# Background ticks of the top-k attention: none in the first maxima pass of the plain attention, more in the wide attention

## The chip, the cores and the metric

One core of a Trainium2 chip runs the whole program. The metric is the device time of one execution in microseconds (us), less is better. The engines are TensorE (PE in the profile, its weight loads PEld), VectorE (DVE), ScalarE (ACT), GpSimd (POOL) and SyncE (SP), which issues most DMAs.

## The reference

Input are 4 batches of 1024 rows of 256. Two layers follow, each `x + ga * attention(norm(x) ...)` and `x + gb * ffn(norm(x) ...)` with a modulation per batch:

```python
# layer 0 attention: 16 heads of 16, causal, each row keeps its 32 largest scores
vals, idx = jax.lax.top_k(scores, K_S)
masked = jnp.put_along_axis(jnp.full_like(scores, -jnp.inf), idx, vals, axis=-1, inplace=False)
attn = jax.nn.softmax(masked, axis=-1)
# layer 0 ffn: 8 experts of 256 x 256, one chosen per row
# layer 1 attention: 16 heads of 64, causal ("wide")
# layer 1 ffn: a plain causal attention, 16 heads of 16, then a sparse mixture
x = x + attention(layernorm(x, ln1_w), c_attn_w, c_proj_w)
x = x + moe_mlp(layernorm(x, ln2_w), router_w, w1, w2)     # 2 of 8 experts per row
```

## The kernel before

All four batches go through one after the other. Each batch b has the foreground stages, in this order: projection and norm of layer 0's attention output, `ffn`, `wide` (8 groups of 2 heads, 16 units of 128 queries by one head in each), `prep` (projection, norms, `project_narrow` for the plain attention), `flip` (the plain attention), its projection, then `moe`.

The top-k attention `topk(b + 1)` of the **next** batch runs in the background. It is a generator on each engine with 472 ticks: 64 steps p of 7 ticks each, and 3 more. In a step DVE takes the 32 largest of 9 x 128 columns with four MAX8 and three MATCH_REPLACE8 for each of two parts (L1497, L1511; one MAX8 pair or one replace pair in a tick), POOL masks (L1866, L1871), ACT copies and takes exponentials (L1133, L1139, L1145), PE computes scores, transposes and values (L459, L470, L485). On DVE step p begins at tick 7(p + 1), so the first seven ticks of a topk hold nothing there. SP's part is staging at ticks that are multiples of 56.

Each foreground stage calls `at(name, i)` at its places; `beside` then advances the generator to the tick that `Pace` has computed for that place, on that engine. The order of instructions on each engine is therefore fixed when the program is built: an engine works in order, and semaphores join the engines. `Pace.STAGES` gives each stage its number of places and its share of the 472 ticks. Batch 3 has nothing in the background (`ticks` is None), so its stages show the foreground alone.

`flip` has a first maxima pass: for head group 0, 32 units `scores_for_max(0, u)` on PE (L666, L668) into the two PSUM buffers pA, and `row_max(0, u)` on DVE (L1658), then `turn_maxima(0)` (L675), `rows_high` on ACT (L1254), `rows_low` on DVE (L1666), and the copies of the two rows nmh and nml into the staged operands by SP (L971, L972). Then come 4 groups of 12 steps. Each step has four `scores_across` on PE (L700, L703), exponentials on ACT (L1282), `values` (L715), and among them the maxima of the next group.

PE's first `scores_across` of a group waits for the landing of nmh and nml. On SP the same queue has, ahead of these two, the staging of groups 1 and 2, twelve copies at L925, which begin when `parts2` has landed:

```python
for g in (1, 2):
    staged(stage2[g][0:KROWS], parts2, g, 0, 4, s["st%d" % g])
for i in range(8):
    at("flip", i)
maxima_rows(0)
```

`staged` makes, for each of two sides, three copies from RUNS: (row, n, first, repeats), n outermost, each row 8 KB:

```python
RUNS = (((0, 3, 0, True), (48, 2, 1, True), (80, 1, 2, True)),
        ((0, 3, 0, False), (48, 2, 0, False), (80, 1, 0, False)))
```

Line numbers below are those of the kernel before.

Of the kernel before, what the change touches and what calls it, by code (L numbers as in the profile page):

```python
# [120 lines left out]
FL = Flip()  # L121
# [19 lines left out]
class Pace:  # L141


    STAGES = (("wide", 8 * 17, 0.49), ("prep", 12, 0.04), ("flip", 8 + 48, 0.22), ("route", 6, 0.06),
              ("moe", 23, 0.13), ("collect", 6, 0.06))

    def __init__(self):
# [41 lines left out]
def build(nc, x, ct, wmod, wqkv, bqk, bv, wo, bo, ffn_wg, ffn_bg, ffn_we, ffn_be, ln_w, router_w, w1, w2, out):  # L189
    ctx = ExitStack()  # L190
    with ctx:
# [195 lines left out]
        def _(pe):  # L387
# [262 lines left out]
            def flip(b, at):  # L650
# [69 lines left out]
                pe.wait_ge(s["d0"], (b + 1) * 192)  # L720
                for u in range(FL.UNITS):
                    scores_for_max(0, u)
                    if u % 4 == 3:
                        at("flip", u // 4)
                turn_maxima(0)
                for g in range(G):
                    for n in range(FL.STEPS):
                        units = FL.units_of(n)
                        for j in range(4):
                            scores_across(g, n, j)  # L730
                            if j % 2 == 0:
                                continue
                            for u in units[0:2] if j == 1 else units[2:4]:
                                if u == FL.LATE and g:
                                    spread_sums(g - 1)
                                if g + 1 < G:
                                    scores_for_max(g + 1, u)
                        if n == 8 and g + 1 < G:
                            turn_maxima(g + 1)
                        if n or g:  # L740
                            values(g if n else g - 1, n - 1 if n else FL.STEPS - 1)
                        at("flip", 8 + 12 * g + n)
                values(G - 1, FL.STEPS - 1)
                spread_sums(G - 1)
                pe.wait_ge(s["mf"], (b + 1) * FL.slots)
# [81 lines left out]
            for b in range(B):  # L827
                at = beside(topk(b + 1) if b + 1 < B else None)
# [22 lines left out]
        def _(sp):  # L851
# [23 lines left out]
            for lo in range(0, SM.TILES * P, N):  # L875
                n = min(N, SM.TILES * P - lo)
# [87 lines left out]
            def flip(b, at):  # L964
                s = a2
                G = FL.GROUPS

                def maxima_rows(g):
                    sp.wait_ge(s["mf"], b * FL.slots + FL.at["turn", g] + 1)
                    sg = stage2[g % 3]  # L970
                    sp.dma_start(sg[96:97, 0, :, :], nmh[:, :]).then_inc(s["md"], 16)  # L971
                    sp.dma_start(sg[97:98, 0, :, :], nml[:, :]).then_inc(s["md"], 16)  # L972

                sp.wait_ge(pj[2]["dr"], (b + 1) * 192)
                sp.wait_ge(a2["d0"], (b + 1) * 192)
                sp.wait_ge(pj[2]["pj"], b * 2 + 2)
                for g in (1, 2):
                    staged(stage2[g][0:KROWS], parts2, g, 0, 4, s["st%d" % g])
                for i in range(8):
                    at("flip", i)  # L980
                maxima_rows(0)
                for g in range(G):
                    for n in range(FL.STEPS):
                        if n == 2 and g == 1:
                            filled(("x", b, 0, 11, 3))
                            staged(stage2[0][0:KROWS], parts2, 3, 0, 4, s["st3"])
                        if n == 9 and g + 1 < G:
                            maxima_rows(g + 1)
                        at("flip", 8 + 12 * g + n)

            def experts(those):
                for e in those:
# [46 lines left out]
            for b in range(B):  # L1039
                at = beside(topk(b + 1) if b + 1 < B else None)  # L1040
# [33 lines left out]
        def _(act):  # L1074
# [170 lines left out]
            def flip(b, at):  # L1245
                s = a2

                def rows_high(g):
                    c = FL.at["turn", g]
                    act.wait_ge(s["mt"], b * FL.GROUPS + g + 1)  # L1250

                    if b or g:
                        act.wait_ge(s["md"], (b * FL.GROUPS + g) * 32)
                    act.activation(nmh[:, :], pA[c % 2][0:32, 0:P], ACT.Copy).then_inc(s["mh"], 1)  # L1254

                def out_of_psum(g, half):
                    act.wait_ge(s["pv"], (b * FL.GROUPS + g) * FL.STEPS + (4 if half == 0 else 12))
                    act.activation(oall2[g][:, half * 512:half * 512 + 512], pV[:, :], ACT.Copy).then_inc(s["o"], 1)

                for i in range(8):  # L1260
                    at("flip", i)
                def sums_columns(g):
                    act.wait_ge(s["o"], (b * FL.GROUPS + g) * 2 + 2)
                    for j in range(4):
                        act.dma_start(rsb2[32 * g + 8 * j:32 * g + 8 * j + 8, :],
                                      oall2[g][32 * j + 16:32 * j + 17, :]).then_inc(s["sd"], 16)

                rows_high(0)
                for g in range(FL.GROUPS):
                    for n in range(FL.STEPS):  # L1270
                        half, kb, q0, w = FL.step(n)
                        now = (b * FL.GROUPS + g) * FL.STEPS + n
                        off = q0 - half * 512
                        if n == 1 and g:
                            out_of_psum(g - 1, 1)
                        if n == 5:
                            out_of_psum(g, 0)
                        if now >= 2:
                            act.wait_ge(s["pv"], now - 1)
                        for j in range(4):  # L1280
                            r = filled(("x", b, g, n, j))
                            act.activation(prT2[:, n % 2, j, off:off + w], r[:, 0:w], ACT.Exp).then_inc(s_re, 1)  # L1282
                        if n == 2 and g:
                            sums_columns(g - 1)
                        if n == 9 and g + 1 < FL.GROUPS:
                            rows_high(g + 1)
                        at("flip", 8 + 12 * g + n)
                out_of_psum(FL.GROUPS - 1, 1)
                sums_columns(FL.GROUPS - 1)

# [78 lines left out]
        def _(v):  # L1369
# [280 lines left out]
            def flip(b, at):  # L1650
                s = a2
                G = FL.GROUPS

                def row_max(g, u):
                    i, j = u // 4, u % 4
                    c = FL.at["max", g, u]
                    v.wait_ge(s["sm"], (b * G + g) * FL.UNITS + u + 1)
                    v.tensor_reduce(nmx[:, j, i:i + 1], pA[c % 2][:, 0:(i + 1) * P], AX, ALU.max, negate=True)\  # L1658
                     .then_inc(s["mf"], 1)

                def rows_low(g):
                    c = FL.at["turn", g]
                    v.wait_ge(s["mh"], b * G + g + 1)
                    if b or g:
                        v.wait_ge(s["md"], (b * G + g) * 32)
                    v.tensor_tensor(nml[:, :], pA[c % 2][0:32, 0:P], nmh[:, :], ALU.subtract).then_inc(s["mf"], 1)  # L1666

                def inverse(g):
                    v.wait_ge(s["sd"], (b * G + g + 1) * 64)
                    rows = slice(32 * g, 32 * g + 32)  # L1670
                    v.reciprocal(rinv2[rows, :], rsb2[rows, :]).then_inc(s["ri"], 1)

                def normalise(g):
                    c = FL.at["sum", g]
                    v.wait_ge(s["bc"], b * G + g + 1)
                    v.wait_ge(s["o"], (b * G + g) * 2 + 2)
                    v.tensor_tensor(oall2[g], oall2[g], pA[c % 2][:, :], ALU.mult).then_inc(s["mf"], 1)

                for u in range(FL.UNITS):
                    row_max(0, u)  # L1680
                    if u % 4 == 3:
                        at("flip", u // 4)
                rows_low(0)
                for g in range(G):
                    for n in range(FL.STEPS):
                        for u in FL.units_of(n):
                            if u == FL.LATE and g:
                                inverse(g - 1)
                                normalise(g - 1)
                            if g + 1 < G:  # L1690
                                row_max(g + 1, u)
                        if n == 8 and g + 1 < G:
                            rows_low(g + 1)
                        at("flip", 8 + 12 * g + n)
                inverse(G - 1)
                normalise(G - 1)

# [104 lines left out]
        def _(pool):  # L1802
# [103 lines left out]
            def flip(b, at):  # L1906
# [10 lines left out]
                    pool.wait_ge(a2["on"], b * 3 + sg)  # L1917
                    pool.memset(stage2[sg][96:98, 1, :, :], 1.0).then_inc(a2["on"], 1)
                pool.wait_ge(a2["on"], b * 3 + 3)
                for i in range(8 + 12 * FL.GROUPS):  # L1920
                    at("flip", i)

            def moe(b, at):
# [126 lines left out]
```

## Time and profile before

| what | value |
| --- | --- |
| median of 3 runs | 6109.72 us (6103.54 to 6121.14) |
| the profiled execution | 6109.4 us |
| its span | 6107.6 us |
| PE, DVE, ACT, POOL busy | 74%, 67%, 45%, 31% |
| granted clock of TensorE, mean | 0.855 |

In the windows of the rows below, the stages of batch 0 are wide 949.8 to 1495.9, first maxima pass 1596.9 to 1640.2, gap to the first maximum of pass 1, steps 1647.1 to 1915.7; of batch 3 in the same order 5207.7, 5686.0, 5712.5 and 5744.6 to 5911.4.

The span is the time from the first to the last instruction of the profiled execution; what lies around it is 1.8 us. Busy time is a mean over stages whose limits differ, so each stage is read in its own window. A bracket such as [5.34 <-DMA SC<-nml] is the idle time of the engine before the instruction and what ended it.

### The profile page before, as it was taken

How to read it: one execution, taken by the hardware profiler on the slowest of the kernel's cores; microseconds unless marked ns; L12 is line 12 of the kernel's file. 1: busy time of each engine (PE TensorE's matmuls, PEld its weight loads, DVE VectorE, ACT ScalarE, POOL GpSimd, SP SyncE). 2: the span in 40 equal slices, each digit the busy share in tenths (PEclk: the TensorE clock that was granted, in tenths of full speed). 3: DMA queues.
4: the chain of work that ended last, by engine and by line, in shares of the span. 5: the costliest groups of instructions: out<-in, count | busy, mean ns of one | idle time of the engine just before them, and what ended most of it. 6: DMA issues, size and time to landing. Idle time of an engine off the chain costs nothing. (4 is left out here: it accounts for less than half of the span.)

```text
span 6107.6 us, 83052 instructions
## 1 busy us (share of the span) xinstructions
PE 4512.7 (74%) x30341; PEld 2897.9 (47%) x30341; DVE 4110.7 (67%) x8455; ACT 2746.5 (45%) x6035; POOL 1905.5 (31%) x1563
## 2 busy tenths in 40 slices
PE   4444478888676858888677658988777577998676
PEld 2333345656333544666433444666533454666334
DVE  5999957777885656777786656877787655223530
ACT  2334315665343623666344541666445350553333
POOL 2555512343323421343322430343333440000001
PEclk7665689999787979999888879999878788999788
DMA  3000000000102020000202120000021111000212
GB/s 120 11 11 25 1 21 27 15 15 11 51 17 88 30 83 24 12 13 9 55 22 68 41 80 33 12 13 12 15 61 34 63 41 38 12 10 13 56 60 72
DMA packets 106730, 213.54 MB, mean 35 GB/s; under 512 B 19128, under 2 KB 64032, under 8 KB 102952
## 3 DMA queue, kind: packets, MB, share of 16 engines
q1 hardware_dynamic: 98136, 190.91, 9.9%
q0 software_dynamic: 6144, 16.79, 0.9%
q8 instruction: 247, 4.05, 0.3%
q14 instruction: 155, 1.27, 0.1%
q10 hardware_dynamic: 2048, 0.53, 0.0%
HBM read 154.38 MB, written 49.73 MB: 33 GB/s over the span
## 5 line engine op out<-in xcount | busy, mean ns | idle before, releaser
L1497 DVE MAX8 vals<-work 128x8 f32<-128x128 f32 (+7 forms) x1536 | 1080.6, 743 | 0.4
L1866 POOL TENSOR_SCALAR keep<-ssb,vals 128x128 bf16<-128x128 f32 (+7 forms) x512 | 876.5, 1724 | 0.0
L470 PE MATMUL ring<-ident,pr 128*128 128x128 f32 x2304 | 487.7, 333 | 488.3 <-POOL pr L1871 439.4
L1511 DVE MATCH_REPLACE8 work<-vals,work 128x128 f32<-128x128 f32 (+7 forms) x1024 | 750.9, 739 | 0.0
L1853 POOL TENSOR_TENSOR pool_step<-ones 128x2 f32<-128x2 f32 x256 | 50.0, 195 | 2242.8 <-DVE vals L1497 2242.1
L577 PE MATMUL pA<-SC 128*128 128x512 f32 (+3 forms) x1536 | 625.0, 517 | 140.9 <-ACT SC L1206 116.0
L1871 POOL TENSOR_TENSOR pr<-keep,pr 128x128 f32<-128x128 bf16 (+7 forms) x512 | 648.2, 1289 | 0.0
L470 PEld LDWEIGHTS ring<-ident,pr 128*128 128x128 f32 x2304 | 334.6, 170 | 642.6 <-POOL pr L1871 466.7
L1145 ACT ACTIVATE prT<-ring 128x512 f32<-128x512 f32 (+1 forms) x768 | 380.4, 496 | 541.1 <-PE ring L470 533.0
L1626 DVE TENSOR_REDUCE nmax<-pA 128x1 f32<-128x1024 f32 (+7 forms) x512 | 382.5, 750 | 258.5 <-PE pA L578 247.4
L1497 DVE MAX8 vals<-ssb 128x8 f32<-128x128 f32 (+7 forms) x512 | 362.9, 750 | 282.9 <-ACT ssb L1133 266.5
L1133 ACT ACTIVATE ssb<-ring 128x512 f32<-128x512 f32 (+3 forms) x768 | 378.6, 494 | 231.1 <-PE ring L462 211.1
L1206 ACT ACTIVATE SC<-pA,nmax 128x1024 f32<-128x1024 f32 (+7 forms) x512 | 381.4, 745 | 174.4 <-DVE nmax L1626 173.4
L1139 ACT ACTIVATE pr<-ssb,nmx 128x128 f32<-128x128 f32 (+7 forms) x512 | 368.1, 768 | 196.4 <-DVE nmx L1504 165.2
L1658 DVE TENSOR_REDUCE nmx<-pA 128x1 f32<-128x896 f32 (+7 forms) x512 | 358.9, 750 | 111.1 <-PE pA L668 108.6
L577 PEld LDWEIGHTS pA<-SC 128*128 128x128 f32 x1536 | 261.5, 194 | 321.0 <-ACT SC L1206 142.3
L1282 ACT ACTIVATE SC<-ring 128x512 f32<-128x512 f32 (+3 forms) x768 | 325.4, 497 | 192.5 <-PE ring L700 95.3
L1215 ACT ACTIVATE SC<-ring 128x512 f32<-128x512 f32 (+3 forms) x768 | 349.7, 491 | 134.7 <-PE ring L586 130.4
L459 PE MATMUL ring<-stage 96*128 96x512 bf16 (+3 forms) x768 | 297.9, 389 | 131.1 <-issue 56.0
L485 PE MATMUL ring<-prT,vall 128*32 128x128 f32 x4608 | 347.4, 317 | 47.6 <-ACT prT L1145 47.4
L1511 DVE MATCH_REPLACE8 work<-vals,ssb 128x128 f32<-128x128 f32 (+7 forms) x512 | 380.9, 750 | 0.0
L1846 POOL TENSOR_TENSOR rstd<-ve,mhalf 128x4 f32<-128x4 f32 x48 | 50.5, 1054 | 1047.4 <-DVE ve L1417 1047.4
(224 smaller groups left out, 8270.5 us busy)
## 6 DMA issues: line engine op xcount, KB each, us to landing
SC<-in_w SPq DMA_DIRECT2D x64, 512.0 KB, 8.2
parts<-SC SPq DMA_DIRECT2D x72, 256.0 KB, 2.4
SC<-in_wqkv SPq DMA_DIRECT2D x32, 384.0 KB, 2.9
stage<-parts SPq DMA_DIRECT2D x64, 192.0 KB
rows_out<-SC SPq DMA_DIRECT2D x92, 128.0 KB, 1.7
SC<-rows_in SPq DMA_DIRECT2D x20, 512.0 KB, 3.9
SC<-parts SPq DMA_DIRECT2D x24, 384.0 KB
stage<-parts SPq DMA_DIRECT2D x64, 128.0 KB
```

The lines of the kernel that those rows point to most:

```text
L470: mm = pe.transpose(r[:, blk % 4 * P:blk % 4 * P + P], pr0[:, p % 2, blk * P:blk * P + P], ident[:, :])
L577: pe.matmul(p[:, lo:hi], qm[:, j, i * P:i * P + P], kT[:, lo:hi], start=True, stop=(hi < w))
L1133: act.activation(ssb0[:, p % 2, col:col + k1 - k0], r[:, 0:k1 - k0], ACT.Copy).then_inc(s_re, 1)
L1139: act.activation(pr0[:, p % 2, lo:hi], ssb0[:, p % 2, lo:hi], ACT.Exp, bias=nmx0[:, p % 2, i:i + 1]).then_inc(s["e"], 1)
L1145: act.activation(prT0[:, p % 2, 4 * c:4 * c + n, :].rearrange("p a n -> p (a n)"), r[:, 0:n * P], ACT.Copy).then_inc(s_re, 1)
L1206: act.activation(pr[:, u % 2, 0:w], pA[(u + 1) % 2][:, 0:w], ACT.Exp, bias=nmax[:, u % 4:u % 4 + 1], accum_out=rsum[:, G % 2, u:u + 1]).th ...
L1497: m = v.max(vals0[:, y, i, 8 * n:8 * n + 8], src[:, lo:hi])
L1511: done[i] = cht.mark(v.match_replace(out=work0[:, lo:hi], in_to_replace=vals0[:, y, i, 8 * n:8 * n + 8], in_values=src[:, lo:hi], imm_valu ...
L1626: v.tensor_reduce(nmax[:, u % 4:u % 4 + 1], pA[(u + 1) % 2][:, 0:w], AX, ALU.max, negate=True).then_inc(s["mx"], 1)
L1658: v.tensor_reduce(nmx[:, j, i:i + 1], pA[c % 2][:, 0:(i + 1) * P], AX, ALU.max, negate=True)\
L1866: pool.tensor_scalar(keep0[:, lo:hi], ssb0[:, p % 2, lo:hi], vals0[:, p % 2, i, TOPK - 1:TOPK], None, ALU.is_ge).then_inc(s["k"], 1)
L1871: pool.tensor_tensor(pr0[:, p % 2, lo:hi], keep0[:, lo:hi], pr0[:, p % 2, lo:hi], ALU.mult).then_inc(s["p"], 1)
```

## The change

Places of `flip` go from 56 to 48: the eight in the first maxima pass (one after every four units) are taken out on all five engines. The share of `wide` goes from 0.49 to 0.53, that of `flip` from 0.22 to 0.18. In ticks (rounded as `Pace` does): wide ends at tick 250 instead of 231, prep at 269 instead of 250 (19 ticks both), the first maxima pass has none instead of 15 (250 to 265), the 48 steps have 85 (269 to 354) instead of 89 (265 to 354). From tick 354 on everything is as before. `wide` keeps its 136 places.

```diff
-    STAGES = (("wide", 8 * 17, 0.49), ("prep", 12, 0.04), ("flip", 8 + 48, 0.22), ("route", 6, 0.06),
+    STAGES = (("wide", 8 * 17, 0.53), ("prep", 12, 0.04), ("flip", 48, 0.18), ("route", 6, 0.06),
               ("moe", 23, 0.13), ("collect", 6, 0.06))
...
# PE
                 for u in range(FL.UNITS):
                     scores_for_max(0, u)
-                    if u % 4 == 3:
-                        at("flip", u // 4)
                 turn_maxima(0)
...
-                        at("flip", 8 + 12 * g + n)
+                        at("flip", 12 * g + n)
...
# SP
                     staged(stage2[g][0:KROWS], parts2, g, 0, 4, s["st%d" % g])
-                for i in range(8):
-                    at("flip", i)
                 maxima_rows(0)
...
# ACT
-                for i in range(8):
-                    at("flip", i)
...
# DVE
                 for u in range(FL.UNITS):
                     row_max(0, u)
-                    if u % 4 == 3:
-                        at("flip", u // 4)
                 rows_low(0)
...
# POOL
-                for i in range(8 + 12 * FL.GROUPS):
+                for i in range(12 * FL.GROUPS):
                     at("flip", i)
```

## Rows read from the trace of the kernel before

**Rows 1.** The page: span and busy shares.

```profile
span 6107.6 us, 83052 instructions
...
PE 4512.7 (74%) x30341; PEld 2897.9 (47%) x30341; DVE 4110.7 (67%) x8455; ACT 2746.5 (45%) x6035; POOL 1905.5 (31%) x1563
```

**Rows 2.** Windows: stretch, us, busy PE, PEld, DVE, ACT, POOL, PEclk, DMA share, GB/s.

```profile
949.80:1495.90 546.10, 482.26 (x3847) 333.98 (x3844) 424.13 (x817) 351.66 (x825) 207.85 (x165) 0.97 0.05 14
2378.10:2921.40 543.30, 477.82 (x3846) 331.00 (x3844) 424.55 (x817) 351.17 (x825) 207.88 (x165) 0.98 0.05 15
...
5207.70:5597.70 390.00, 372.36 (x2776) 250.35 (x2773) 108.11 (x144) 229.96 (x551) 16.44 (x7) 1.00 0.04 11
1596.90:1640.20 43.30, 28.11 (x145) 14.36 (x145) 42.18 (x74) 8.71 (x17) 17.65 (x12) 0.62 0.20 70
1640.20:1647.10 6.90, 2.05 (x10) 0.98 (x10) 2.92 (x7) 1.90 (x5) 0.00 (x0) 0.50 0.06 21
1647.10:1915.70 268.60, 199.38 (x1625) 96.55 (x1622) 206.23 (x374) 135.06 (x310) 79.15 (x65) 0.86 0.14 44
...
5686.00:5712.50 26.50, 21.83 (x78) 6.56 (x76) 22.86 (x32) 0.00 (x0) 7.01 (x2) 0.51 0.29 98
5712.50:5744.60 32.10, 1.86 (x9) 1.02 (x10) 0.28 (x1) 0.92 (x3) 0.00 (x0) 0.50 0.13 48
5744.60:5911.40 166.80, 135.28 (x1197) 57.18 (x1195) 76.33 (x107) 84.57 (x202) 0.00 (x0) 0.93 0.17 61
```

**Rows 3.** Timeline of batch 3, end of pass 0.

```profile
5717.61 2.35 SPq L971 DMA_DIRECT2D SC<-nmh  x1
5720.00 0.81 SPq L972 DMA_DIRECT2D SC<-nml  x1
5743.13 0.10 PEld L700 LDWEIGHTS ring<-SC 98*128 98x128 bf16 x1 [30.51 <-DMA SC<-nml]
```

**Rows 4.** Source view of L972, the copies of nml, all batches.

```profile
  PE ring L700: 47.2, 4
...
DMA to landing us min/median/max: 1.9/1.9/23.1
```

**Rows 5.** DMA view, 5736 to 5742.2: queue, packets, MB, share of 16.

```profile
q1 hardware_dynamic: 22, 0.16, 6.3%
```

**Rows 6.** Timeline and SP's waits, batches 0 and 2: L925, L972, first L700.

```profile
1595.35 25.70 SPq L925 DMA_DIRECT2D SC<-parts  x12
1643.76 0.59 SPq L972 DMA_DIRECT2D SC<-nml  x1
1645.67 0.61 PE L700 MATMUL ring<-SC 98*128 98x512 bf16 x1 [4.85 <-DMA SC<-nml]
...
SPq L925 <- DMA parts<-SC: 3.1, 1, 3.1
...
4445.98 26.58 SPq L925 DMA_DIRECT2D SC<-parts  x12
4493.05 0.59 SPq L972 DMA_DIRECT2D SC<-nml  x1
4496.94 0.61 PE L700 MATMUL ring<-SC 98*128 98x512 bf16 x1 [6.83 <-DMA SC<-nml]
```

**Rows 7.** Windows of wide groups: batch 1's first, second, last; batch 3's.

```profile
2379.20:2440.30 61.10, 56.19 (x437) 38.22 (x437) 46.86 (x92) 41.79 (x97) 20.65 (x16) 1.00 0.07 20
2440.30:2510.80 70.50, 62.00 (x488) 42.48 (x488) 54.40 (x108) 44.34 (x104) 26.72 (x21) 0.98 0.06 19
...
2792.40:2866.80 74.40, 62.14 (x489) 42.97 (x489) 54.63 (x106) 44.68 (x105) 28.68 (x24) 0.98 0.01 2
5208.90:5259.40 50.50, 48.35 (x360) 32.53 (x360) 13.47 (x19) 29.43 (x70) 2.35 (x1) 1.00 0.03 10
```

**Rows 8.** Source views of L1626 and L1282: counts, first and last start.

```profile
L1626 DVE TENSOR_REDUCE nmax<-pA x512: 271/786/1226, 951.0 to 5594.7; 128x1 f32<-128x384 f32 x22, 128x1 f32<-128x1024 f32 x22, 128x1 f32<-128x256 f32 x22, 128x1 f32<-128x128 f32 x21
...
L1282 ACT ACTIVATE SC<-ring x768: 271/573/667, 1646.4 to 5895.7; 128x512 f32<-128x512 f32 x96, 128x384 f32<-128x384 f32 x32, 128x256 f32<-128x256 f32 x32, 128x128 f32<-128x128 f32 x32
```

More of the change, by code:

```diff
@@ L988, in flip @@
                             maxima_rows(g + 1)
-                        at("flip", 8 + 12 * g + n)
+                        at("flip", 12 * g + n)
             def experts(those):
@@ L1286, in flip @@
                             rows_high(g + 1)
-                        at("flip", 8 + 12 * g + n)
+                        at("flip", 12 * g + n)
                 out_of_psum(FL.GROUPS - 1, 1)
@@ L1693, in flip @@
                             rows_low(g + 1)
-                        at("flip", 8 + 12 * g + n)
+                        at("flip", 12 * g + n)
                 inverse(G - 1)
```

## The prediction

> **What bounds the kernel now.** I read the page first. The span is 6107.6 us and no engine is near full over it: PE 74%, DVE 67% [rows 1]. So the share of the span says nothing here, and the stages have to be read one by one.
>
> The stage windows come next [rows 2]. The wide attention of batch 3, which carries no background, takes 390.0 us with PE busy 372 of it: that stage is TensorE's. With 231 background ticks beside it (batches 0 to 2; rows stand for two of the three, the third lies between) it takes 546.1 and 543.3 us, PE 480 and DVE 424 busy. Neither is full, so part of the stretch is waiting: DVE works in order, and a row maximum of the foreground stands behind whichever ticks come before it. The steps of the plain attention take 268.6 us with 89 ticks (batches 1 and 2 within 3.3 us of it), 166.8 us without.
>
> The stretch that the change empties is the first maxima pass. With its 15 ticks it takes 43.3 us, DVE busy 42.2 of them (batches 1 and 2 within 1 us). Batch 3 has no ticks: 26.5 us, DVE 22.9 [rows 2]. Read alone, this promises 16 to 17 us a batch. But the window behind it turns that round: 6.9 us with ticks (up to 8.5), 32.1 us without. From the first maximum of pass 0 to the first of pass 1 it is 50.2 us with ticks and 58.6 us without them. The batch that is free of ticks is the slowest.
>
> The timelines say why. In batch 3 the pass ends, the rows nmh and nml are sent, and PE stands still for 30 us, released by the landing of nml [rows 3]. That landing took 23.1 us, where the least and the middle one of all 16 are 1.9 [rows 4]. In front of these two small copies on SP's queue are the twelve copies L925 (stage2 of groups 1 and 2, 3 MB). SP itself was held up in issuing them until 5717.6 [rows 3]. At the end of this transfer one DMA engine alone is at work: 6.3% of 16 engines is one of 16, and 0.16 MB in 6.2 us is one packet of 8 KB each 0.31 us [rows 5].
>
> In batches 0 and 2 the L925 copies are issued from 1595.35 and 4445.98, and L700 starts at 1645.67 and 4496.94 [rows 6]: 50.3 and 51.0 us after the first issue (53.8 in batch 3, from 5689.34). The nml copy was issued only at 1643.76 and 4493.05, so it took 1.9 and 3.9 us to release PE. The first is the bare landing, the second is already held up; batch 1 lies between with 2.4. So with ticks the pass ends just where the staged transfer ends. Its ticks are free.
>
> **The change part by part.**
>
> *Pass 0 loses 15 ticks* (250 to 265 of 472). On DVE that is 42.2 - 22.9 = 19.3 us, on ACT 8.7, on POOL 10.6, on PE 6.3 [rows 2]; on SP none (it stages at ticks 224, 280 and 336, all outside). Of this, the path gets back what lies after the end of the transfer: 0 us (batches 1 and 2), at most 0.3 (batch 0). What hides it is the transfer L925; if that cover were gone, the pass would be 26.5 + 6.9 = 33.4 us and the gain 16.8. The transfer starts after the landing of parts, for which SP waits 3.1 us [rows 6], which the change leaves alone; nmh and nml would be issued near 1624 and then wait as in batch 3. The bound on the other side is batch 3's 53.8 us against 50.3: a loss of 3.5. I take 0, the value of the three batches that have the same neighbours.
>
> By the Trainium skill (DMA: Bandwidth & Descriptors, Rules for kernel authors) a copy whose outermost dimension is c < 16 is confined to c engines. The runs of L925 have 3, 2 and 16 outermost, so the first engine would carry 16 + 16 + 1 rows of each of four sides, 132 packets; at the 0.31 us that the row shows [rows 5] that is an estimate of 41 us, and the last packet would come some 6 us before the trace has it. By that floor the change would gain 6 us a batch more than I count. The trace agrees with the one busy engine at the end, and not with so early an end.
>
> *The wide attention gains 19 ticks* (231 to 250). Its 136 places hold 41 single ticks and 95 doubles now, and would hold 22 and 114: nineteen places go from one tick to two. Price from below: the mean over the stage, (544.7 - 390.0) / 231 = 0.67 us a tick; PE's own part of that is (480 - 372) / 231 = 0.47, DVE's 1.37 [rows 2]. From above: the first group has its 29 ticks too, but the first seven of a topk do nothing on DVE. It takes 61.1 us, the second 70.5, the last 74.4, a group without ticks 50.5 [rows 7]. The six later groups of batch 1 average 71.1, from the starts of the row maxima [rows 8]: 10.0 us for seven ticks, 1.4 us each. Between the two, the places themselves: taken over the starts of the 512 row maxima L1626 [rows 8], an interval with one tick is 0.24 us longer than the same one in batch 3 (93 of them), with two ticks 1.45 us (219), a difference of 1.21. A part of that is backlog from the place before. I take 1.1 us, near the place difference since this is the very step that the change makes: 19 x 1.1 = 20.9 us a batch. The bounds are 0.67 and 1.45, the whole of what a double costs: 12.7 to 27.6.
>
> *The 48 steps lose 4 ticks* (89 to 85). Mean price (268.6 - 166.8) / 89 = 1.14 us [rows 2]. By places, from the starts of the exponentials L1282 [rows 8], a double against a single costs 1.65 us in the first three groups, 0.2 in the last. I take 1.4: -5.6 us a batch, bounds -4.6 and -6.6.
>
> *What is shifted.* Prep keeps 19 ticks, two and a half of the 64 steps later. The four small ACT copies of sums (tick 240), the spread (245) and POOL's two products move from prep into the last wide group; DVE's reciprocal, which needs the copies, comes three ticks behind them, one and a half places or some 6 us, against the 2 us that small copies like nml take to land [rows 4]. POOL is busy 208 of 545 us in wide. I cost this at 0. SP's staging at tick 280 goes from step 8 to step 6 of group 0, farther from the maxima rows at step 9; PE waited for those rows four times in all [rows 4], once a batch, each time in pass 0, so 0. Route, experts and collect keep their ticks: the shares before them add up to 0.75 either way. Batch 3 has no background and doesn't change.
>
> *PE's clock.* In pass 0 the granted clock is 0.62, in the gap 0.50, the lower of its two levels (1.2 GHz); in batch 3 0.51 and 0.50 [rows 2]. Pass 0 would be at the lower level, as in batch 3, where it needed 26.5 us, far under the transfer: nothing on the path.
>
> **Sum.** A batch: 0 + 20.9 - 5.6 = +15.3 us. Three batches: +46 us. The profiled execution took 6109.4 us (span 6107.6, with 1.8 around it), the median of the runs is 6109.72, so the profiled execution stands for them. So 6155 us, 0.75% slower. The bounds give (12.7 - 6.6 - 0.3) x 3 = +17 and (27.6 - 4.6 + 3.5) x 3 = +80: 6127 to 6189.
>
> **Rivals.**
> *The pass isn't held by the transfer.* If the staging ended early once DVE was out of its way, the pass would shrink by 16.8 us: -16.8 - 5.6 + 20.9 = -1.5 a batch, 6105 us: not slower. It decides where the wide tick costs under 1.18 us; at the mean price of 0.67 it gives -29 us, 6080. Against it: batch 3 has no ticks and is held 30 us [rows 3]. 5%, half of it faster.
> *The transfer ends at the 41 us of the outermost-dimension rule:* 15.3 - 6 = 9.3 a batch, 6137 us. Against it: the rows end at 50 [rows 6]. 7%, slower.
> *Wide has room.* PE is idle 64 of 545 us and DVE 120 [rows 2]. If the second tick only fills such holes, as the first does at 0.24 us, then 19 x 0.24 = 4.6, and with -5.6 it is -1.0 a batch: 6107 us, no change. Against it: a double is already 1.2 us dearer. 15%, of it 3 faster.
> *The order falls differently.* Groups with the same 29 ticks take from 68.6 to 74.4 us by where the ticks fall [rows 7, 8], and all three batches repeat it. One shift of such size each way, 6 us a batch, is 18 us: 6137 or 6173; this is inside the forecast's own spread. A longer chain in the transfer (3.5 a batch) or a worse order on top passes 6180. 10% for more than +70.
>
> **How the numbers follow.** The forecast (+20 to +70 us) has 63%; its own range is 6130 to 6180. A measurement of this kernel tells about 0.3%, 18 us, from no change. Slower: 63 + 7 + 10 = 80%. Same: 12 from room in wide, 2 from the free pass: 14%. Faster: 6%. The range 6118 to 6192 leaves out the cases near no change and the worst ones, 10% at either end, and holds the bounds of the costs.
>
> **What would show it.** In the profile after: pass 0 at 26 to 28 us in batches 0 to 2, the gap behind it at 23 to 27 us with PE waiting on nml's landing (not 7), their sum still 50 to 54; nml's landing some 20 us in four cases, not one; wide at 558 to 574 us; the steps at 259 to 263. The prediction is wrong if the pass and gap together fall under 45 us, or if wide grows by less than 9 us.

## The result, and the profile after

The changed kernel takes 6164.88 us (median of 4 runs, 6157.13 to 6175.3) against 6111.19 us of the kernel before, run beside it: ratio 1.009, 95% interval 1.0074 to 1.0105. It is slower, by 0.9%. The profiled execution took 6167.22 us, its span is 6165.4 us, 57.8 us above the span of before.

The windows by stage come first: the same five stretches as in [rows 2] (wide, prep, first maxima pass, gap, steps) for batch 1, then pass and gap of batches 0, 2 and 3. Columns are those of [rows 2].

```profile
2404.20:2977.20 573.00, 497.17 (x3950) 341.85 (x3949) 451.36 (x875) 361.02 (x844) 227.64 (x181) 0.95 0.05 14
2977.20:3084.70 107.50, 73.22 (x384) 55.11 (x383) 70.61 (x170) 30.48 (x50) 33.65 (x24) 0.81 0.20 45
3084.70:3111.10 26.40, 21.60 (x76) 6.59 (x76) 22.74 (x33) 0.00 (x0) 2.49 (x1) 0.52 0.22 75
3111.10:3132.30 21.20, 1.89 (x10) 1.05 (x11) 0.28 (x1) 0.95 (x3) 0.00 (x0) 0.50 0.11 43
3132.30:3387.50 255.20, 195.88 (x1581) 91.73 (x1579) 200.83 (x363) 132.30 (x304) 72.94 (x60) 0.86 0.15 47
...
1630.60:1657.00 26.40, 21.61 (x76) 6.61 (x76) 22.73 (x33) 0.00 (x0) 2.53 (x1) 0.52 0.24 74
1657.00:1680.40 23.40, 1.91 (x10) 1.07 (x11) 0.34 (x3) 1.03 (x3) 0.00 (x0) 0.50 0.10 42
...
4525.20:4551.60 26.40, 21.61 (x76) 6.62 (x76) 22.69 (x33) 0.00 (x0) 2.46 (x1) 0.52 0.23 70
4551.60:4577.50 25.90, 1.87 (x10) 1.03 (x11) 0.28 (x1) 0.93 (x3) 0.00 (x0) 0.50 0.10 39
...
5747.70:5774.10 26.40, 21.79 (x77) 6.56 (x76) 22.80 (x32) 0.00 (x0) 7.01 (x2) 0.51 0.30 99
5774.10:5802.10 28.00, 1.90 (x10) 1.06 (x11) 0.32 (x3) 0.96 (x3) 0.00 (x0) 0.50 0.14 54
```

The pass fell from 43 us to 26.4 in each batch, and the gap behind it rose to 23.4, 21.2 and 25.9 us, with PE busy 1.9 us of it. The two together are 49.8, 47.6 and 52.3 us, where they were 50.3, 49.9 and 51.4. The timeline of batch 1 at this place answers to [rows 3] and [rows 6]; the source view of the nml copies (now L970) to [rows 4]:

```profile
3080.09 26.39 SPq L923 DMA_DIRECT2D SC<-parts  x12
3112.19 0.57 SPq L969 DMA_DIRECT2D SC<-nmh  x1
3112.80 0.59 SPq L970 DMA_DIRECT2D SC<-nml  x1
3130.80 0.61 PE L700 MATMUL ring<-SC 98*128 98x512 bf16 x1 [19.25 <-DMA SC<-nml]
...
  PE ring L700: 90.7, 4
```

nml is issued 32.7 us after the first staging copy instead of 47.3, and PE starts 50.7 us after it instead of 49.7 (52.9 and 55.5 in batches 0 and 2, where it was 50.3 and 51.0). PE's waiting for nml went from 47.2 us to 90.7, still four times.

The account of the 57.8 us, from the stage windows of both kernels (batches 0 to 2 summed, the last row batch 3):

| stretch | before, us | after, us | difference |
| --- | --- | --- | --- |
| wide, 231 / 250 ticks | 546.1 543.3 544.5 | 573.3 573.0 572.1 | +84.5 |
| prep, 19 / 19 ticks | 101.0 101.9 101.0 | 107.3 107.5 107.1 | +18.0 |
| pass and gap, 15 / 0 ticks | 50.3 49.9 51.4 | 49.8 47.6 52.3 | -1.9 |
| steps, 89 / 85 ticks | 268.5 265.1 266.7 | 255.8 255.2 253.9 | -35.4 |
| the rest up to the next wide | 462.4 463.2 442.6 | 468.0 458.5 438.0 | -3.7 |
| batch 3, pass and gap; other | 58.6 | 54.4 | -4.2; +0.5 |

Within wide the growth is not even. Wide goes by eight groups of two heads, and the fifth alone (here in batch 1, before and then after) takes some 12 us more; its granted clock there is 0.92 where it was 0.98:

```profile
2647.20:2721.20 74.00, 64.19 (x556) 45.00 (x555) 55.47 (x105) 46.20 (x107) 29.21 (x23) 0.98 0.03 8
...
2687.10:2773.10 86.00, 71.67 (x597) 49.68 (x595) 59.38 (x112) 48.78 (x112) 37.57 (x29) 0.92 0.02 6
```

From the starts of the row maxima, the seven groups that can be bounded changed by +5.8, +2.7, +1.0, +6.2, +11.4, +1.4 and -3.8 us in batch 1, at two to four ticks more in each.

### The profile page after: what moved, and what is told of

Read it like the earlier page. It is cut to its first block and busy times, and to the rows that moved or that the text cites. A ratio compares the mean times of both kernels' runs of the same rounds, so it can differ in the third digit from the quotient of the medians.

```text
span 6165.4 us, 83052 instructions
## 1 busy us (share of the span) xinstructions
PE 4550.0 (74%) x30341; PEld 2898.3 (47%) x30341; DVE 4113.5 (67%) x8455; ACT 2745.0 (45%) x6035; POOL 1902.3 (31%) x1563
## 5 line engine op out<-in xcount | busy, mean ns | idle before, releaser
L586 PE MATMUL ring<-ident,SC 128*128 128x128 f32 x2304 | 349.1, 279 | 35.7 <-ACT SC L1202 32.8
```

The costliest lines, as they stand in the source:

```text
L586: mm = pe.transpose(r[:, kb % 4 * P:kb % 4 * P + P], pr[:, u % 2, kb * P:kb * P + P], ident[:, :])
```

## The experiments

Twelve kernels were run. The kernel before, run beside them, had medians of 6107.01, 6112.22 and 6112.94 us (runs 1 to 4; 6 to 9; 5, 10, 11 and 12). Stage times below are means over batches 0 to 2 of the stage windows, as in the table, unless a batch is named. They are of one profiled execution of each kernel; with the same 231 ticks, wide came out between 541.7 and 549.7 us in single batches, so a difference of a microsecond or two in a stage says little.

**1. Staging spread over the DMA engines, in the changed kernel.**

```diff
+            def staged_16(dst, dram, g, h0, h1, done):
+                for side in range(2):
+                    for t, term in enumerate(TERMS):
+                        sp.dma_start(dst[16 * t:16 * t + 16, side, :, :], dram[side, term[side], g, :, h0:h1, :])\
+                          .then_inc(done, 16)
...
-                    staged(stage2[g][0:KROWS], parts2, g, 0, 4, s["st%d" % g])
+                    staged_16(stage2[g][0:KROWS], parts2, g, 0, 4, s["st%d" % g])
...
-                        pe.wait_ge(s["st%d" % g], (b + 1) * 96)
+                        pe.wait_ge(s["st%d" % g], (b + 1) * 192)
```

The staging of group 3, which goes out in the steps, is cut in the same way.

> The changed kernel, with the staging of stage2 issued as one copy for every 16 rows (outermost dimension 16, twelve copies a group instead of six, the same bytes). Theory (the first maxima pass without ticks is held by the staged transfer, whose last packets go through one DMA engine): the gap behind the pass falls from 21 to 26 us to about 7, pass and gap together from 50 to about 34 in batches 0 to 2 and from 54 to about 34 in batch 3, so 3 x 16 + 20 = 68 us less than the changed kernel: about 6097 us. Rival (nml's landing is late for another cause than this transfer): pass and gap stay at about 50, the time at 6165.

Measured: 6087.41 us median, ratio to before 0.996 (0.9946 to 0.9974), 77 us less than the changed kernel and 10 under the expectation. Batch 1 and batch 3, pass and gap, by the windows, and batch 1 on SP and PE:

```profile
3057.40:3083.80 26.40, 21.61 (x76) 6.59 (x76) 22.71 (x33) 0.00 (x0) 2.44 (x1) 0.52 0.76 94
3083.80:3088.90 5.10, 1.89 (x10) 1.05 (x11) 0.28 (x1) 0.95 (x3) 0.00 (x0) 0.50 0.03 6
...
5692.90:5719.40 26.50, 21.86 (x79) 6.54 (x76) 22.87 (x32) 0.00 (x0) 7.01 (x2) 0.51 0.98 151
5719.40:5725.00 5.60, 1.91 (x10) 1.07 (x11) 0.30 (x2) 0.97 (x3) 0.00 (x0) 0.50 0.23 31
...
3052.74 10.98 SPq L929 DMA_DIRECT2D SC<-parts  x24
3085.49 0.59 SPq L977 DMA_DIRECT2D SC<-nml  x1
3087.41 0.61 PE L700 MATMUL ring<-SC 98*128 98x512 bf16 x1 [3.17 <-DMA SC<-nml]
```

The share of the 16 DMA engines that is busy in the pass is 0.76 where it was 0.22: the same bytes now go through many engines at once and are there before DVE is done. nml is issued 32.75 us after the first staging copy, as in the changed kernel (32.7), and PE starts 1.9 us after it instead of 18.0. The gap falls from 21.2 to 5.1 us, pass and gap to 31.5. The rival is out: it was this transfer that held PE behind the pass. Wide, prep and steps stay as in the changed kernel.

**2. The same staging in the kernel before** (edit as in 1).

> The kernel before, with the same staging in copies of 16 rows. Theory (there DVE with its 15 ticks and the transfer end together): batches 0 to 2 keep 43 us of pass and 7 of gap, only batch 3 falls from 58.6 to about 34 us, so about 25 us less than before: 6086 us. Rival (the transfer is all that holds the pass, ticks or none): all four batches fall by 15 us or more, about 6040 us.

Measured: 6079.98 us, ratio 0.995 (0.9934 to 0.9967). Pass and gap 50.3, 49.4 and 49.5 us in batches 0 to 2, and 31.6 in batch 3. Batch 1, by the windows:

```profile
3019.90:3062.30 42.40, 27.99 (x145) 14.16 (x145) 41.30 (x74) 8.70 (x17) 17.86 (x12) 0.66 0.56 72
3062.30:3069.30 7.00, 2.14 (x11) 1.06 (x11) 2.94 (x8) 1.92 (x5) 0.00 (x0) 0.50 0.01 2
```

With ticks, DVE fills the time whether the transfer is there or not; so in the kernel before both ended nearly together, as read from [rows 6]: without the floor it is the same in batch 0, and 0.5 and 1.9 us shorter in batches 1 and 2. With the floor gone the changed kernel really has its 18 us a batch (31.5 against 49.7), and even then it is not faster than this one: 6087 against 6080.

**3. The fifteen ticks to the steps instead of wide.**

```diff
-    STAGES = (("wide", 8 * 17, 0.53), ("prep", 12, 0.04), ("flip", 48, 0.18), ...
+    STAGES = (("wide", 8 * 17, 0.49), ("prep", 12, 0.04), ("flip", 48, 0.22), ...
```

> The changed kernel with the old shares (wide 0.49, flip 0.22): the 15 ticks of the first maxima pass go to the 48 steps (104 instead of 89), none to wide. Theory: pass and gap together stay at 50 us (held by the transfer), wide at 544 and prep at 102 us as before, and the steps grow by 15 ticks. At the mean price of before, 1.14 us, that is +17 us a batch (6162 us); at the price that the changed kernel showed when it took 4 ticks away, 12 us for 4 or 3.0 each, it is +45 us a batch (6245 us). Rival (pass 0 gives back its 17 us): near 6110 us.

Measured: 6154.28 us, ratio 1.0068 (1.0051 to 1.0084). Wide 546.5, prep 101.1, pass and gap 55.5, 49.5 and 49.2, steps 283.2. The steps of batch 1:

```profile
3104.20:3386.70 282.50, 207.49 (x1693) 100.56 (x1690) 227.06 (x420) 143.72 (x329) 91.23 (x75) 0.86 0.13 42
```

They are 16.5 us over before for 15 ticks, 1.1 each, the mean price. The 3.0 us that the change seemed to get back for each of its four was not a price of ticks. The 15 ticks that the pass had for nothing cost 47 us in all when the steps take them.

**4. The shares alone, the places in the pass kept.**

```diff
-    STAGES = (("wide", 8 * 17, 0.49), ("prep", 12, 0.04), ("flip", 8 + 48, 0.22), ...
+    STAGES = (("wide", 8 * 17, 0.53), ("prep", 12, 0.04), ("flip", 8 + 48, 0.18), ...
```

> The kernel before with the shares alone changed (wide 0.53, flip 0.18), its eight places in the first maxima pass kept: 250 ticks in wide, 19 in prep, 12 in the pass, 73 in the steps. Theory: wide 573 and prep 107 us as in the changed kernel (same ticks at the same places), pass and gap still about 50 us though 12 ticks are back in it, and the steps, with 12 ticks fewer than in the changed kernel, 14 us (1.14 each) to 36 us (3.0 each) a batch less than its 255: 6123 to 6057 us. Rival (the ticks in the pass cost what they take on DVE, 1.3 us each): pass and gap 15 us longer, so 45 us above that.

Measured: 6157.41 us, ratio 1.0073 (1.0056 to 1.0089). Wide 573.4 and prep 107.3, the changed kernel's to a tenth or two, steps 239.7 (73 ticks; 1.3 us a tick under its 255.0). But pass and gap came out at 58.8, 62.8 and 59.6 us, which neither theory had (50 and 65); the time is 34 us above the theory's range and inside the rival's, but not by the rival's reason. The windows and the timeline of SP in batch 1 give the reason:

```profile
3077.70:3117.10 39.40, 25.21 (x104) 11.92 (x104) 38.07 (x67) 6.78 (x14) 13.00 (x10) 0.60 0.21 68
3117.10:3140.50 23.40, 1.93 (x10) 1.09 (x11) 1.87 (x6) 0.98 (x3) 1.67 (x2) 0.50 0.12 44
...
3073.10 28.73 SPq L925 DMA_DIRECT2D SC<-parts  x12
3111.07 13.86 SPq L925 DMA_DIRECT2D stage<-parts  x6
3124.97 0.68 SPq L971 DMA_DIRECT2D SC<-nmh  x1
3125.70 0.74 SPq L972 DMA_DIRECT2D SC<-nml  x1
```

With these shares tick 280 falls into the pass. That is the tick at which SP stages the next heads of the top-k; its six copies were issued ahead of nmh and nml and held SP for 13.9 us, so nml went out only 52.6 us after the first staging copy, and PE started 13.3 us after that. The tick is free on DVE and dear on SP's queue; how much of it is SP's being held and how much the six copies' own transfer was not taken apart.

**5. As 4, with tick 280 outside the pass.**

```diff
-    STAGES = (("wide", 8 * 17, 0.49), ("prep", 12, 0.04), ("flip", 8 + 48, 0.22), ...
+    STAGES = (("wide", 8 * 17, 0.52), ("prep", 12, 0.04), ("flip", 8 + 48, 0.19), ...
```

> The kernel before with the shares wide 0.52 and flip 0.19, places as before: 245 ticks in wide, 13 in the first maxima pass (264 to 277), 77 in the steps. Here the pass does not hold tick 280, the one at which SP stages the next pair of heads for the top-k, ahead of nmh and nml. Theory (in shares_only the gap behind the pass was 20 us because that staging stood in SP's queue ahead of the rows): pass 40 us, gap about 10, together 50. Rival (13 ticks in the pass shift the transfer itself): together 59 or more as in shares_only.

Measured, a single run: 6078.57 us. Pass and gap, batch 1, by the windows:

```profile
3025.80:3067.90 42.10, 28.38 (x138) 14.25 (x138) 40.73 (x71) 8.00 (x16) 19.15 (x12) 0.58 0.21 71
3067.90:3078.30 10.40, 1.91 (x10) 1.07 (x11) 1.63 (x5) 0.97 (x3) 0.00 (x0) 0.50 0.08 32
```

52.5, 52.5 and 51.1 us with 13 ticks, against 47.6 to 52.3 with none: the theory, and not the rival's 59. From the first staging copy to L700 it is 49.9, 49.8 and 48.8 us, less than in the changed kernel: thirteen ticks cost nothing there. Wide is 559.2 (245 ticks), prep 97.7, steps 247.4 (77). That this kernel came out 34 us under the runs of before beside it rests on a single run, and isn't claimed.

**6. Half of the way.**

```diff
-    STAGES = (("wide", 8 * 17, 0.53), ("prep", 12, 0.04), ("flip", 48, 0.18), ...
+    STAGES = (("wide", 8 * 17, 0.51), ("prep", 12, 0.04), ("flip", 48, 0.20), ...
```

> The changed kernel with wide 0.51 and flip 0.20: 241 ticks in wide, 19 in prep, none in the pass, 94 in the steps. Theory (a wide tick over 231 costs about 1.5 us, since each one turns a single place into a double): wide near 559 us, midway between 544.7 and 572.8; steps at 1.1 to 1.4 us a tick over the changed kernel's 255, so 266 to 268; pass and gap 50. Time about 6160 us. Rival (what wide gained is a matter of where the ticks fall, not of their number): wide anywhere from 544 to 575 and not between.

Measured: 6139.02 us, ratio 1.0042 (1.0026 to 1.0059). Wide of batch 1:

```profile
2384.30:2943.20 558.90, 491.36 (x3898) 337.93 (x3895) 435.80 (x847) 356.58 (x835) 218.67 (x174) 0.96 0.05 15
```

The mean of wide is 558.1, just between; the time is 21 us under the expectation, to which the steps (263.4) add some, as does prep (105.1, against 107.3 in the changed kernel). With the runs above and the last one below, wide takes 523.5, 544.6, 558.1, 559.2 and 572.8 us with 212, 231, 241, 245 and 250 ticks. More ticks make it longer at every step: 1.11 us each from 212 to 231 and 1.48 from 231 to 250. But it is no straight line: from 241 to 245 ticks it grows by 1 us, from 245 to 250 by 14. So where the ticks fall has a part of several microseconds too, and the rival isn't out altogether.

**7. The nineteen ticks in prep.**

```diff
-    STAGES = (("wide", 8 * 17, 0.53), ("prep", 12, 0.04), ("flip", 48, 0.18), ...
+    STAGES = (("wide", 8 * 17, 0.49), ("prep", 12, 0.08), ("flip", 48, 0.18), ...
```

> The changed kernel with wide 0.49, prep 0.08, flip 0.18: the 19 ticks that the change adds to wide stand in prep (38 in its 12 places). Theory (a foreground on DVE's path pays a tick's DVE time in full, 1.3 to 1.6 us): wide back to 545, prep from 107 to about 133, steps 255, so much the same as the changed kernel, 6160 us. Rival (prep has room, since without any tick it takes 88 and with 19 only 101): prep near 114 us, about 6110 us.

Measured: 6141.69 us, ratio 1.0054 (1.0035 to 1.0072). Prep, pass and gap of batch 1:

```profile
2945.80:3077.80 132.00, 81.04 (x491) 61.52 (x487) 104.01 (x227) 39.51 (x68) 51.80 (x39) 0.83 0.17 41
3077.80:3104.40 26.60, 21.75 (x76) 6.68 (x76) 22.77 (x33) 0.00 (x0) 4.53 (x2) 0.50 0.18 71
3104.40:3120.10 15.70, 1.90 (x10) 1.06 (x11) 0.28 (x2) 0.96 (x3) 0.00 (x0) 0.50 0.10 42
```

Prep is 132.2 us, 31 more than before for 19 ticks (1.6 each): the theory. Pass and gap fell to 43.0, though, which made the whole 18 us less than expected. The timelines show why: here the first staging copy stands 7.4 to 7.7 us ahead of the first maximum (4.6 in the changed kernel, 1.0 to 1.5 before): DVE works through MAX8 and MATCH_REPLACE8 instructions of the ticks before its first maximum, while the staging is already under way. From that copy to L700 it is 48.5 to 49.8 us, within what it took elsewhere.

**8 and 9. Both kernels without the replacements.** MATCH_REPLACE8 is left out of the background on DVE in both, so the four MAX8 read the same scores and the 32nd largest isn't found.

```diff
-                    src = ssb0[:, y, :] if n == 0 else work0[:, :]
+                    src = ssb0[:, y, :]
...
                         if r % 2 == 0:
                             maxima(p - 1, r // 2)
-                        else:
-                            replace(p - 1, r // 2)
```

> The kernel before without the MATCH_REPLACE8 instructions of the background (three of seven ticks are then empty on DVE; the 32nd largest score is no longer found, the four MAX8 read the same scores, so the output differs). It is the base for the next run. Theory: wide and the steps fall by DVE's share, wide to about 470 us, steps to about 220; the first maxima pass falls to about 36 us and the gap grows, pass and gap staying at 50 us. Rival (PE's or ACT's part of a tick sets wide): wide stays above 520.

> The changed kernel without the same MATCH_REPLACE8 instructions. Theory (the price of the 19 added ticks in wide is DVE's time in front of the row maxima): wide is only 9 to 14 us above the run before it instead of 28, and the whole time 10 to 25 us above it instead of 58. Rival (PE and the shared ring of PSUM banks set the price): wide is still 28 us above it.

Measured, a single run each: 5782.67 and 5860.56 us. Wide of batch 1, first in the one, then in the other:

```profile
2173.00:2692.20 519.20, 470.76 (x3815) 326.44 (x3812) 295.80 (x433) 347.80 (x820) 207.54 (x165) 0.99 0.05 15
```

```profile
2203.30:2747.80 544.50, 486.04 (x3951) 336.16 (x3949) 308.42 (x459) 359.38 (x844) 227.66 (x181) 0.97 0.05 15
```

DVE lost 128 us of 424 and wide only 24 of 545; the expectation of 470 us for wide missed, and the rival's, above 520, came true. The step from one share to the other costs 26.0 us in wide (520.6 to 546.6), nearly the whole 28.2, though the added ticks now take 13 us of DVE and not 27. My theory expected 9 to 14 and fell: the price of the added ticks is hardly DVE's time. The whole times are 78 us apart, where 10 to 25 was expected. PE's added busy time is 16 us in either pair. The fifth group is again where most of it arises: in batch 1 it takes 69.8 and then 83.5 us, at a granted clock of 1.00 and 0.92. The same pair shows the floor once more: in the first of them the pass is shortened to 37.5 us by the lighter ticks, the gap grows to 14.9, the sum is 52.4.

**10 and 11. The spread of the sums taken apart.** The waits view of wide, batch 1, named a candidate. First two lines of before, then of after:

```profile
DVE nmax L1626 <- PE pA L578: 31.3, 29, 2.5
ACT rbc L1166 <- POOL oall L1878: 2.7, 1, 2.7
```

```profile
DVE nmax L1620 <- PE pA L578: 37.4, 28, 4.9
ACT rbc L1162 <- POOL oall L1870: 11.2, 2, 5.9
```

ACT's second copy of rbc waits for POOL's product with the first, POOL being busy with a selection. Tick 245, the second such spread, moved from prep into wide; it is the very end of the stage, at 2976 us, and has 5.4 us of the wait. The other 5.9 stand in the fifth group, where before had 2.7.

```diff
-                    if r == 0 and p >= 19 and (p - 19) % 16 == 0:
-                        spread((p - 19) // 16)
+                    if r in (0, 2) and p >= 19 and (p - 19) % 16 == 0:
+                        spread((p - 19) // 16, r // 2)
```

(and likewise `normalise` on POOL; each call does one half.)

> The changed kernel with the spread of the top-k sums taken apart: its second half (PE, ACT, POOL) stands two ticks behind the first instead of right behind it. In the changed kernel ACT waits 11.2 us a batch in wide at the second copy of rbc for POOL's product with the first (2.7 us in the kernel before, where one of the two spreads stands in prep), and the exponentials of wide wait behind it. Theory (this wait is a good part of what the added ticks cost wide and prep): wide falls from 573 to about 565 us, the time by about 25 us to 6140. Rival (the wait is hidden by PE's own work, the price is the mere number of ticks): wide stays at 573.

> The kernel before with the same spread taken apart. Theory: wide falls by 2 to 3 us a batch and prep by 2 to 3, together 15 us of the whole: about 6095 us, so the difference between the two kernels falls from 55 to about 45. Rival: no change, 6110.

Measured: 6160.61 us (ratio 1.008, 1.0063 to 1.0096) and 6104.54 us (0.9986, 0.9976 to 0.9996). The first was expected at 6140 and did not move; the second fell by 8 us and not by 15, and the two are 56 us apart, not 45. Wide of the first is 571.9, one microsecond less. The edit didn't remove the wait, only cut it:

```profile
ACT rbc L1163 <- POOL oall L1871: 8.2, 2, 4.6
DVE nmax L1621 <- PE pA L579: 36.2, 26, 4.3
```

3 us less at this place came with 1 us less in wide, which is inside the scatter of that stage. The theory that this wait is a good part of the price isn't borne out. As the wait was not taken away in full, its whole weight stays open.

**12. Combined.** The kernel before with the staging of 1, the spread of 10, and 19 ticks moved from wide to moe.

```diff
-    STAGES = (("wide", 8 * 17, 0.49), ...  ("moe", 23, 0.13), ("collect", 6, 0.06))
+    STAGES = (("wide", 8 * 17, 0.45), ...  ("moe", 23, 0.17), ("collect", 6, 0.06))
```

> The kernel before with the staging in copies of 16 rows, the spread taken apart, and the shares wide 0.45 and moe 0.17 (212 ticks in wide, 19 more in moe). Theory (a tick in wide costs about 1.4 us at the margin, one in moe about 0.9): wide falls by 27 us a batch and moe grows by 18, besides the 27 us of before_spread and up to 15 of the spread: about 6040 us. Rival (ticks in moe cost as much): 6070.

Measured: 6064.35 us, ratio 0.9921 (0.9904 to 0.9937), the fastest of the repeated ones, 24 us over the theory and 6 under the rival. Wide and steps of batch 1:

```profile
2373.20:2896.30 523.10, 472.04 (x3762) 326.36 (x3759) 394.60 (x761) 340.21 (x800) 193.43 (x153) 0.97 0.05 14
3047.60:3304.80 257.20, 192.96 (x1621) 92.28 (x1618) 202.72 (x375) 135.32 (x310) 75.44 (x62) 0.88 0.15 43
```

Wide falls to 523.5 (-21.1, and not -27), but the rest up to the next wide grows from 456.1 to 483.7, 1.45 us a tick and not 0.9: the rival was right about moe. The steps are 255.7 us with the same number of ticks as before, 89, against 266.8. The spread staging is not the reason, since run 2 has it and takes 265.9; nor are the halves of the spread, since in run 11 the stretch up to the last exponential is as before (249.7 us against 249.2, and 239.6 here). What differs is which ticks stand there (246 to 335 in place of 265 to 354). That is eleven microseconds by the order.

## Why the prediction was right

The time was forecast at 6155 us, 46 above; it came at 6165, 54 above. The mechanism that decides the direction, free ticks in the pass against dear ticks in wide, is right. That the size came so near is partly luck: three of the four terms lay off by 6 to 7 us a batch, outside their bounds or where I had given none, and half of it cancelled. Per batch, by the prediction's own steps:

- *Pass 0: 0 us, its ticks free.* Measured -0.6, and from the first staging copy to L700 +2.7, inside the bound of 3.5 (4.5 in batch 2). That the ticks were free is shown from three sides: with the transfer spread the gap falls to 5.1 us (1), under the transfer as it was 13 ticks can be put back for nothing (5), and lighter ticks lengthen the gap by no less than they shorten the pass (8). Over all runs and batches in which PE waited for the unspread transfer (run 4 apart), it was 48.5 to 57 us from the first staging copy to L700, and it differed so even between batches of one kernel (55.4, 49.2 and 48.7 us in run 3); why is open. In batch 1 that made the gap 21.2 and the sum 47.6 us, both under the ranges I had named for them (23 to 27, 50 to 54).
- *The outermost dimension.* Run 1 shows that it matters: outermost 16 in place of 3 and 2 took the DMA share in the pass from 0.22 to 0.76. The 41 us that I estimated for one engine stayed under the 50 that the rows had, and the rows were right for the time: the shortest of all was 48.5.
- *Wide: 19 ticks at 1.1 us.* Measured 28.2 us, 1.48 each, just over the upper bound of 27.6. This term was under-sized by 7. The difference that I read between places with one and two ticks, 1.21, was nearer, and I went below it for a backlog. The price is a mean: 11.4 us of it arise in the fifth group of batch 1, and by run 5 it isn't even from tick to tick.
- *Its cause.* I took DVE's queue for the reason, since a row maximum stands behind the ticks. Runs 8 and 9 contradict that for most of it. What else in a tick costs wide is open: PE's own share is 16 us of busy time (480 to 496), of which 9 would be 19 ticks at 0.47. The granted clock is lower too, 0.97 before and 0.95 after, and lowest in the two groups that grew most (0.91 and 0.92 in the fourth and fifth of batch 1, both 0.98 before); whether the clock lengthened these groups, or waits there lowered the clock, no run tells. The weight of the spread's wait is open. No run took PE's or ACT's part of a tick away.
- *Prep: 0.* Measured +6.0. This was the step that failed. Prep has 19 ticks in all of before, after and runs 3 to 6, and takes from 97.7 to 107.3 us in the mean. Kernels with the same ticks there agree (101.3 and 101.1 with ticks 231 to 250, 107.3 three times with 250 to 269), so which ticks meet the projection matters more than I allowed. About 3 of the 6 us fall behind the start of the staging, where the transfer covers them.
- *Steps: -5.6.* Measured -11.8, far outside the bounds of -4.6 and -6.6. With 73, 77, 85, 94 and 104 ticks the steps follow a fitted line of 1.3 us a tick within 4 us (239.7 to 283.2), near my price of 1.4; the kernel before, with 89, lies 6 us above that line, and run 12 with 89 lies 5 below it. So the other half of the gain goes with the order of the ticks in the kernel before, not with their number.
- The misses in size, +13 us in wide and prep and -6 in the steps, cancel to half. The forecast of a slower kernel didn't need them to. The rest up to the next wide, which I took as unchanged, gave 3.7 us back over three batches; no run tells why.
- *Batch 3, clock, SP's staging: 0.* Batch 3 gave 4 us in the same transfer. The pass stood at the lower clock level (0.52) without effect. That tick 280 is harmless held for this change, and run 4 shows how near it was.

## What to carry to other kernels

Before work is taken out of a stretch, look for a stretch of the same kernel that already lacks it and add the gap behind it: a stage whose end waits for a transfer gives nothing back, and the best place for background work is beside such a transfer. It is worth looking at a copy whose outermost dimension is small: here, cutting the staging into copies with 16 outermost alone took the kernel before from 6107 to 6080 us. Where background instructions are woven into a foreground by hand, more of them cost more (1.1 to 1.5 us each in the mean here), but their order adds or takes up to ten microseconds a stage, so a change of the one should be read apart from the other.

## What the hardware showed that I had not expected

Leaving out 128 of 424 us of VectorE work in wide shortened that stage by 24 us only, though VectorE had been busy for 78% of it. TensorE's granted clock in wide was 0.97 before and 0.95 with more background in the same stage; where VectorE's part was left out of the kernel before it was 0.99 in two batches of three. The six copies that SyncE issued behind the staged transfer in run 4 held it for 13.9 us; in run 1 all 24 smaller ones went out in 11.0 us, where the twelve before them took 26.4. In the changed kernel the nml copy of 8 KB landed in 18.0 to 22.8 us when it was issued behind the unspread transfer, and in 1.9 us in the median of all 16.
